# Border tiles first in the logit pass, and a weighted pass with four buffers, in a graph network on one Trainium2 core

## The reference

```python
q, k, v = (x @ Wq + bq), (x @ Wk + bk), (x @ Wv + bv)      # each (n, 8, 16)
e = (edge_attr @ We).reshape(-1, H, C)
alpha = einsum('ehc,ehc->eh', q[dst], k[src] + e) / sqrt(C)
amax = segment_max(alpha, dst, num_segments=n)
ex = exp(alpha - amax[dst])
denom = segment_sum(ex, dst, num_segments=n)
msg = (v[src] + e) * (ex / (denom[dst] + 1e-16))[:, :, None]
out = segment_sum(msg, dst, num_segments=n)
```

## Time and profile before

| | |
|---|---|
| median of 3 runs | 4402.17 us (4401.73 to 4405.57) |
| the profiled execution | 4408.67 us, span 4406.8 us, mean granted TensorE clock 0.815 |
| busy, share of the span | TensorE 65%, its weight loads 49%, VectorE 42%, ScalarE 10%, GpSimd 61% |
| logit pass | 3468 to 4001 us |
| segment max | 4001 to 4090 us |
| splitting | 4090 to 4112 us |
| weighted pass | 4112 to 4298 us |

### The profile page before, as it was taken

One profiled execution on the slowest core, in us unless ns is written; L12 is line 12 of the kernel. 1 busy time (PEld: TensorE's weight loads), 2 busy tenths in 40 slices (PEclk: granted clock), 3 DMA queues, 4 the chain that ended last, 5 costly groups with the idle time before them and its releaser, 6 DMA issues. The chain is left out here.

```text
span 4406.8 us, 65487 instructions
## 1 busy us (share of the span) xinstructions
PE 2876.3 (65%) x12218; PEld 2170.9 (49%) x12219; DVE 1830.9 (42%) x4838; ACT 421.2 (10%) x690; POOL 2678.7 (61%) x2816
## 2 busy tenths in 40 slices
PE   6555675555765568666677777766557665662687
PEld 3444444444444444444446666544444555652574
DVE  4222252222522226444453333422223666668764
ACT  2000020000200002000021111210001111110334
POOL 3777737777377773777727777367774477771000
PEclk9777797777977779778779999877777888886899
DMA  6222222222222222222212222122221355551340
GB/s 181 55 55 55 53 84 55 55 54 52 84 55 55 54 52 83 55 55 54 52 31 52 52 52 52 27 58 55 55 53 32 104 154 156 156 156 47 114 133 15
DMA packets 157822, 314.71 MB, mean 71 GB/s; under 512 B 58069, under 2 KB 79004, under 8 KB 157086
## 3 DMA queue, kind: packets, MB, share of 16 engines
q0 software_dynamic: 95744, 209.89, 18.4%
q1 hardware_dynamic: 55454, 101.15, 6.6%
q10 hardware_dynamic: 6400, 1.65, 0.2%
HBM read 250.84 MB, written 61.64 MB: 71 GB/s over the span
## 5 line engine op out<-in xcount | busy, mean ns | idle before, releaser
L595 POOL DMA_INDIRECT ring<-m_tab,idx x1568 | 1488.6, 949 | 720.1 <-issue 601.0
L1480 PE MATMUL ps<-oh,ring 128*128 128x256 f32 (+1 forms) x3328 | 963.6, 451 | 485.7 <-DMA ring<-m_tab,idx 380.6
L1480 PE MATMUL ps<-nodes,ring 128*128 128x256 f32 x2350 | 808.5, 509 | 475.1 <-DMA ring<-m_tab,idx 363.3
L1480 PEld LDWEIGHTS ps<-oh,ring 128*128 128x128 f32 x3328 | 703.2, 241 | 630.8 <-issue 528.0
L595 POOL DMA_INDIRECT ring<-x_tab,idx x795 | 754.9, 950 | 254.7 <-issue 244.3
L1480 PEld LDWEIGHTS ps<-nodes,ring 128*128 128x128 f32 x2350 | 575.6, 259 | 617.2 <-issue 516.4
L1018 DVE TENSOR_SCALAR oh<-iota,dl 128x256 f32<-128x256 f32 x1248 | 380.2, 375 | 951.4 <-PE ps L1480 943.3
L1018 DVE TENSOR_SCALAR nodes<-iota,dl 128x256 f32<-128x256 f32 x1183 | 361.8, 376 | 831.6 <-PE ps L1480 829.0
L595 POOL DMA_INDIRECT ring<-kv_tab,idx x416 | 399.2, 960 | 148.7 <-issue 126.5
L605 POOL TENSOR_TENSOR small<-small,bc 128x4 f32<-128x4 f32 (+1 forms) x28 | 31.1, 1109 | 597.4 <-DVE small L1118 597.4
L1480 PE MATMUL ps<-wpad,rts 128*128 128x128 f32 x832 | 162.8, 376 | 195.9 <-DVE pw L1270 195.9
(11 more groups left out here) (248 smaller groups left out, 2432.1 us busy)
## 6 DMA issues: line engine op xcount, KB each, us to landing
ring<-m_tab SPq DMA_DIRECT2D x2560, 0.5 KB
ring<-m_tab ACTq DMA_DIRECT2D x2560, 0.5 KB
ve_dr<-pw SPq DMA_DIRECT2D x52, 512.0 KB, 2.9
ring<-ve_dr SPq DMA_DIRECT2D x52, 512.0 KB, 3.4
ring<-m_tab,idx POOLq DMA_INDIRECT x1572, 2.6
m_tab<-ring SPq DMA_DIRECT2D x75, 256.0 KB, 2.2
ring<-x_tab,idx POOLq DMA_INDIRECT x796, 2.4
ring<-x_tab SPq DMA_DIRECT2D x640, 0.5 KB
```

The source lines that it names most:

```text
L595: pool.indirect_dma_start(rows[:, j, :], None, table, bass.IndirectOffsetOnAxis(ap=idx[:, g * WV + j:g * WV + j + 1], axis=0)).then_inc(ga ...
L1480: return T.matmul(o, lhsT, rhs, start=start, stop=stop, skip_group_check=True)
```

## The change

- **Order of the logit pass.** The waves 48 to 51, which hold the border copies, come first, written out (`logit_turns`); the loop then runs over waves 0 to 47. `alE` is filled with zeros first, and VectorE adds the scaled logits to what is there. At the end of each turn of the loop VectorE reads two tile numbers and adds two border slots to their tiles, in place of the 24 additions behind the loop. All engines and the gathers follow the new order.
- **Turned-over logits** are copied out of PSUM by ScalarE (`t_a`, `t_b`), and VectorE only scans. Eight fills become two of one column.
- **The weights of the border slots** are copied by GpSimd, behind its gathers; the last turn of the weighted pass waits for them (`ex_x`).
- **Splitting** is done turn by turn inside the weighted pass, for 32 slots, one turn ahead, in two buffers (`ex_parts`, `ex_rest1`, `ex_rest2`). ScalarE's copy of a wave's parts is gone. The reload of v + e waits for the last transposes of the weights only.
- **Weighted pass**: four buffers of one-hots and of their bf16 copies (`b_hot`, `ohb`); one-hots of a wave wait for the wave four before it. TensorE reads the sixteen column numbers of a wave from one row (`cols_b`, `load_both`). The loop's body holds two turns; the last three turns are written out. The two operations for `wbeta` stand behind the pass.

```diff
--- before.py
+++ after.py
@@ -88,10 +88,17 @@
...
+def load_both(pe, row, wave):
+
+    return pe.bass.values_load_multi_w_load_instructions(
+        row[0:1, ds(wave * (2 * WV), 2 * WV)], engines=[mybir.EngineType.PE], min_val=0, max_val=NP + (WIN - 1) * 24,
+        skip_runtime_bounds_check_because="window starts are multiples of 128 under 3200 by construction")[1]
...
@@ -182,9 +189,10 @@
...
-        cols24 = sb("cols24", [1, SLOTS], I32)
+        cols_b = sb("cols_b", [1, 2 * SLOTS], I32)
         tix = sb("tix", [1, 2 * EXTRA], I32)
-        basef = sb("basef", [1, SLOTS])
+        basef = cols_b[:, 0:SLOTS].bitcast(F32)
+        cols_v, cols_d = (cols_b[:, :].rearrange("p (g k j) -> p g k j", k=2, j=WV)[:, :, k, :] for k in range(2))
...
@@ -362,11 +375,11 @@
...
-        ohb = (pw[:, 2:4, :].rearrange("p a b -> p (a b)").bitcast(BF16)
-               .rearrange("p (b s c) -> p b s c", b=2, c=P))
+        ohb = (pw[:, :, :].rearrange("p a b -> p (a b)").bitcast(BF16)
+               .rearrange("p (b s c) -> p b s c", b=RING, c=P))
+        b_hot = ([oh[:, b, :, :] for b in range(2)]
+                 + [yT[:, 1024 * b:1024 * (b + 1)].rearrange("p (s c) -> p s c", c=P) for b in range(2)])
...
@@ -430,6 +443,25 @@
...
+
+        def logit_turns(eng, body):
+
+            for u in range(RING):
+                body(0, u, WAVES - RING + u)
+            with eng.Fori(0, TURNS - 1) as i:
+                for u in range(RING):
+                    body(i + 1, u, i * RING + u)
+
+        def weigh_turns(body):
+
+            def run(eng):
+                with eng.Fori(0, TURNS // 2 - 1) as i:
+                    for par in range(2):
+                        body(i * 2 + par, par, False)
+                for t in range(TURNS - 3, TURNS):
+                    body(t, t % 2, t == TURNS - 1)
+
+            return run
 
...
@@ -530,16 +562,16 @@
...
-            sp.wait_ge(s_dv, DV["ex_done"])
+            sp.wait_ge(s_pe, PE[f"exE{HEADS - 1}"])
...
@@ -583,18 +615,19 @@
...
+                    wave = (g - RING) % WAVES if single(k) else g
...
@@ -619,6 +652,15 @@
...
+            pool.wait_ge(s_dv, DV[f"ex{EX_DV - 1}"])
+            pool.wait_ge(s_ac, AC[f"ex{HEADS - 1}"])
+            for i in range(EXTRA // WV):
+                t = load_tiles(pool, tix, i, mybir.EngineType.Pool)
+                for j in range(WV):
+                    nc.gpsimd.tensor_copy(alE[:, i * WV + (TILES + j):i * WV + (TILES + j + 1), :],
+                                          alE[:, ds(t[j], 1), :]).then_inc(ex_x, 1)
+            nc.gpsimd.tensor_copy(alE[:, TILES + EXTRA:SLOTS, :], alE[:, 0:SLOTS - TILES - EXTRA, :]).then_inc(ex_x, 1)
...
@@ -771,16 +813,22 @@
...
+            act.wait_ge(s_dv, DV["t_z"])
+            for h in range(HEADS):
+                act.wait_ge(s_pe, PE[f"alT{h}"])
+                step(f"t_a{h}", nc.scalar.activation(alT[:, h * 512:h * 512 + 384], ps[:, h, 0:384], ACT.Copy))
+                step(f"t_b{h}", nc.scalar.activation(alT[0:TILES % P, h * 512 + 384:(h + 1) * 512],
+                                                     ps[0:TILES % P, h, 384:512], ACT.Copy))
...
@@ -790,20 +838,28 @@
...
+            def ex_parts(t, par):
+
+                if not isinstance(t, int) or t:
+                    act.wait_ge(b_used, t * RING)
+                if isinstance(t, int) and t == TURNS - 1:
+                    act.wait_ge(ex_x, EXTRA + 1)
+                nc.scalar.activation(ex3w[:, par, :, 0, :], alE[:, ds(t * TURN_S, TURN_S), :], ACT.Copy).then_inc(b_e0, 1)
+                act.wait_ge(b_r1, t + 1)
+                nc.scalar.activation(ex3w[:, par, :, 1, :], ex_rest[:, par, :, :], ACT.Copy).then_inc(b_e1, 1)
...
+            def weigh(t, par, last):
                 for u in range(RING):
-
-                    act.wait_ge(b_oh, i * RING + (u + 1))
-                    nc.scalar.activation(ex3w[:, u % 2, :, :], ex3f[:, ds((i * RING + u) * WV, WV), :], ACT.Copy)
-                    nc.scalar.activation(ohb[:, u % 2, :, :], oh[:, u % 2, :, :], ACT.Copy).then_inc(b_ohb, 1)
+                    act.wait_ge(b_oh, t * RING + (u + 1))
+                    nc.scalar.activation(ohb[:, u, :, :], b_hot[u], ACT.Copy).then_inc(b_ohb, 1)
+                if not last:
+                    ex_parts(t + 1, 1 - par)
+
+            ex_parts(0, 0)
+            weigh_turns(weigh)(act)
...
@@ -1245,69 +1303,75 @@
...
+            V.memset(alE[:, :, :], 0.0).then_inc(a_out, 1)
...
-                    V.tensor_scalar(alE[:, ds((i * RING + u) * WV, WV), :],
-                                    red[:, v, :].rearrange("p (s h) -> p s h", h=HEADS), 1.0 / HC ** 0.5, None,
-                                    ALU.mult).then_inc(credit, 1)
...
+                sums_ = alE[:, ds(wave * WV, WV), :]
+                dve.wait_ge(a_red, t * RING + (u + 1))
+                dve.wait_ge(a_v, g2 + 3)
+                if u == 0 and not isinstance(t, int):
+                    dve.wait_ge(a_out, t * 2)
+                elif isinstance(t, int):
+                    dve.wait_ge(a_out, 2)
+                V.scalar_tensor_tensor(sums_, red[:, v, :].rearrange("p (s h) -> p s h", h=HEADS), 1.0 / HC ** 0.5, sums_,
+                                       ALU.mult, ALU.add).then_inc(credit, 1)
+                if u == RING - 1 and not isinstance(t, int):
+                    tiles = load_tiles(dve, tix, t - 1, n=2)
+                    for j in range(2):
+                        if j == 0:
+                            dve.wait_ge(credit, (t + 1) * RING + before)
+                        dve.wait_ge(a_out, t * 2 + j)
+                        V.tensor_tensor(alE[:, ds(tiles[j], 1), :], alE[:, ds(tiles[j], 1), :],
+                                        alE[:, ds(t * 2 + (TILES + j - 2), 1), :], ALU.add).then_inc(a_out, 1)
...
-            for j, op in enumerate((ALU.add, ALU.subtract)):
-                step(f"wb{j}", V.tensor_tensor(wbeta[:, j, :], b_(f"L3_wbeta{j}").to_broadcast([P, P]),
-                                               b_("L3_wbeta2").to_broadcast([P, P]), op))
-
-            with dve.Fori(0, EXTRA // WV) as i:
-                t = load_tiles(dve, tix, i)
-                for j in range(WV):
-                    dve.wait_ge(a_out, i * WV + (j + 1))
-                    V.tensor_tensor(alE[:, ds(t[j], 1), :], alE[:, ds(t[j], 1), :],
-                                    alE[:, ds(i * WV + (TILES + j), 1), :], ALU.add).then_inc(a_out, 1)
-            dve.wait_ge(a_out, EXTRA + 1)
...
-                dve.wait_ge(s_pe, PE[f"alT{h}"])
-                step(f"t_a{h}", V.tensor_copy(alT[:, h, 0:384], ps[:, h, 0:384]))
-                step(f"t_b{h}", V.tensor_copy(alT[0:LAST, h, 384:512], ps[0:LAST, h, 384:512]))
-                after(f"t_b{h}")
+                dve.wait_ge(s_ac, AC[f"t_b{h}"])
...
@@ -1321,8 +1385,8 @@
...
-            for j in range(4, 12):
-                step(f"c_i{j}", V.memset(L8[j], -BIG))
+            step("c_if", V.memset(cf[:, 0:1], -BIG))
+            step("c_ib", V.memset(cb[:, 511:512], -BIG))
...
@@ -1372,31 +1436,45 @@
...
+            def ex_rest1(t, par):
+                if not isinstance(t, int) or t:
+                    dve.wait_ge(b_e2, t)
+                if isinstance(t, int) and t == TURNS - 1:
+                    dve.wait_ge(ex_x, EXTRA + 1)
+                dve.wait_ge(b_e0, t + 1)
+                V.tensor_tensor(ex_rest[:, par, :, :], alE[:, ds(t * TURN_S, TURN_S), :], ex3w[:, par, :, 0, :],
+                                ALU.subtract).then_inc(b_r1, 1)
+
+            def ex_rest2(t, par):
+                dve.wait_ge(b_e1, t + 1)
+                V.tensor_tensor(ex3w[:, par, :, 2, :], ex_rest[:, par, :, :], ex3w[:, par, :, 1, :],
+                                ALU.subtract).then_inc(b_e2, 1)
...
+            def weigh(t, par, last):
...
-                    g = i * RING + u
-                    sl = ds(g * WV, WV)
-                    dve.wait_ge(b_used, g + (RING - 1))
-                    one_hot(PASS_L3, i, u).then_inc(b_oh, 1)
-                    dve.wait_ge(b_ld[u], (i + 1) * 16)
+                    g = t * RING + u
+                    dve.wait_ge(b_used, g + 1)
+                    for j in range(0, WV, 2):
+                        ins = V.tensor_tensor(b_hot[u][:, j:j + 2, :], iota.unsqueeze(1).to_broadcast([P, 2, P]),
+                                              dl[:, ds(g * WV + j, 2)].unsqueeze(2).to_broadcast([P, 2, P]),
+                                              ALU.is_equal)
+                    ins.then_inc(b_oh, 1)
+                    if u == 0:
+                        ex_rest2(t, par)
+                    dve.wait_ge(b_ld[u], t * 16 + 16)
                     vv = ring[:, u, 0:WV // 2, :].rearrange("p a (s c) -> p (a s) c", c=HC)
-                    V.tensor_tensor(vv, vv, alE[:, sl, :].rearrange("p s h -> p (s h)").unsqueeze(2)
+                    V.tensor_tensor(vv, vv, alE[:, ds(g * WV, WV), :].rearrange("p s h -> p (s h)").unsqueeze(2)
```

(29 more changed lines are left out.)

198 lines of the change are left out of this document (92 added, 106 removed).

## The result

| | before | after |
|---|---|---|
| median of 4 runs of each | 4403.03 us (4401.73 to 4405.57) | 4359.51 us (4354.99 to 4362.24) |
| ratio | | 0.9899, 95% interval 0.9882 to 0.9917 |
| profiled execution: its own time, span | 4408.7, 4406.8 us | 4361.1, 4359.3 us |
| first gather of the logit pass starts | 3468.5 | 3468.9 |
| last scaling starts | 4001.1 | 4005.0 |

The prediction was 4330 us, with a range from 4318 to 4354. The two profiled executions are 47.5 us apart, and the timeline of after says where each part of that lies. Its columns are those of the earlier trace rows: start, duration, engine, line, operation, idle before.

The account below looks back on a forecast made before the run. GpSimd's issue bounds the logit pass, a VectorE chain the segment-max stretch, TensorE's queue the weighted pass. Terms -12.1 - 5.2 - 0.5 - 17.9 - 37.0 = -72.7 us give 4336 from the profiled 4408.7, 4330 by the median; range 4318 to 4354.

Parts of the forecast that it names:

- the load of sixteen numbers: TensorE's queue, weighted pass: one load per wave, 0.70 us at worst by 14 ns a number, 0.59 if count doesn't matter.
- the 2.79 us: Weighted pass: time TensorE's array alone needs for a wave, about 0.93 + 1.86.
- p = 3.47 less 0.74 for one load: Weighted pass: wave time p falls from 3.47 us by 0.74 for one load less; p taken as 2.83.
- The start of the pass: Weighted pass: first three waves run partly at a granted clock of 0.50, adding 2.2 us.
- The fill in the logit pass: Start of logit pass: zeroing the weights falls where VectorE waits for gathers; price 0, at most 3.0 us.
- the tail: After the logit pass's last wave: scaling-and-adding, one load and two additions replace the 24 additions; -12.1 us.
- the short chain: After the scans: fills shrink from eight to two of one column, but TensorE's transposes come late next; -0.5 us.
- the splitting: From ScalarE's last weights to the first small product: small product starts at about 4094.1 us; -17.9 us.
- the column numbers: Setup operations, two fewer and three more elsewhere, stand beside other work or waits: 0, bounds -0.7 and +0.5 us.
- Two loads stay: Rival, weighted pass: sixteen numbers need two loads of eight; term -3 instead of -37, time 4363 us; chance 11%.
- VectorE held by GpSimd's copies: Rival, weighted pass: GpSimd's 25 copies each hold up VectorE 1.01 us; term -15, time 4352 us; chance 12%.
- Numbers beyond eight one at a time: Rival, TensorE's queue: eight further numbers at 0.49 us each, load 4.5 us, time about 4530 us; chance 2%.

Follow-up runs that it names:

- the best version: Changed kernel with denominators 32 columns apart, eight numbers a wave, TensorE's turns written out, one-instruction one-hots and zeroing by ScalarE: median 4324.6 us, ratio 0.9828 to before.
- the ten loads: Changed kernel plus extra loads of 1 to 16 numbers in TensorE's queue: prices fit 0.06 us plus 0.26 us for each fetch.

## Why the prediction was wrong, by its steps

**The failed step is one term of the sum, the load of sixteen numbers.** It took "14 ns a number" from two rows, one number at 0.49 and eight at 0.59, and got 0.59 to 0.70; it is 1.10. Both rows are right, and the line through them is not: eight numbers are two fetches, and the one-number load is no unit of the same series (another single number took 0.32, so 0.49 held something else). With 0.51 more, the prediction's own lower figure of 2.78 becomes 3.29, and the 171.2 us measured are 52 x 3.29. That the two agree to the hundredth is partly chance: steady waves are 3.25, and the back edges make up the rest. The price was bounded by a straight line through two rows, and the range reached no further than that line. The weighted pass is 21.8 of the 25.2 us that are missing between the profiled executions: 24 from the wave (3.29 for 2.83), less 2.2 for a slow start that did not come.

**The bound was named right, and the 2.79 us beside it was half misread.** "TensorE's queue" gave the wave in every kernel but the two with one column for all small products. The 2.79 us put down to TensorE's array was 0.93 + 1.86. The 0.93 is the pace at which the queue dispatches the small products, which take 0.2 us up to the first large one when nothing holds them up; the 1.86 is real. As the time of a wave on TensorE with changing columns 2.79 was nearly right all the same: the best version has turns of 11.1 us, 2.78 a wave. But the two limits of 2.79 and 2.78 shared the dispatch of the small products, and a run was needed to see that TensorE alone could do 2.25.

**p = 3.47 less 0.74 for one load.** The 0.74 held the load and what stands around it. What the merge really spared was 0.28, the whole way from 3.53 to 3.25; with its two loads the new loop is no faster than the old one at 3.47, so the four buffers added nothing to the steady wave.

**The start of the pass**, +2.2 for the low clock: not seen. The first wave took 4.3 us at a granted clock of 0.50, 1.1 more than a steady one, and the second 2.4, 0.9 less, its numbers having been loaded while the first large products ran.

**The fill in the logit pass**, price 0, "at most 3.0 if it held up GpSimd's first issues": that is what it did, 2.5 us (4.14 to the second gather against 1.62 in before), and the start lay 0.4 later. The place was named and the wrong end taken. The reason given, that VectorE waits there, was about VectorE; the one to ask was GpSimd. The remaining 1.0 us of the +4.0 is spread over 414 gathers; it too is gone in the two traces in which ScalarE zeroes (532.6 us from the first gather to the last scaling in before, 536.1 in after, 532.7 in the last version). How the fill could reach that far the traces don't show, and two traces are few. The border additions in the turns stayed hidden, as said: VectorE still waits 154 us for gathers in the pass.

**What held**: the tail (1.68 us from the scaling to the last addition's end, 1.6 to 1.8 predicted), heads 2.23 us apart (2.25), the short chain, the splitting (first small product 3.64 us after the last weights, 3.9 predicted; first large one 1.03 later), the column numbers at 0.

**The rivals.** *Two loads stay*: there was one, with nearly the price of two; the time of that rival, 4363, was closer than the forecast. *VectorE held by GpSimd's copies*: out. GpSimd was busy 9.7 of the 10 us from 4077 to 4087, and VectorE's operations beside it took 1.42 and 1.22 us as everywhere. The copies took 0.4 us each and not 1.0 to 1.4, and were done by 4087, 140 us before ScalarE first read them. *Numbers beyond eight one at a time*: not so. Even at 0.26 us for each of the eight, the smallest step that the ten loads show, the load would have been 2.7 us, and it is 1.10.

**The two rules.** The Trainium skill, Runtime: NRT & Kernel Launch, section Instruction fetch mechanics, has about 200 ns per register. By the page's terms that is a load of registers from HBM, and the loads here read a row in SBUF, so the prediction applied the rule to a case that the page doesn't name. Sixteen took 1.10 us, 69 ns each, a third of the rule. It was nearer in kind than the prediction's line, since the price does rise with the numbers, but not evenly: fourteen cost more than sixteen. The Trainium skill, SBUF — State Buffer, section SBUF: two separate sides, in its box on DMAs issued by GpSimd, says that such a DMA can't write its descriptors while VectorE runs a fast-mode copy in SBUF. Here it was a fill, which the box doesn't name, and the first gather of 3.84 us beside a fill of 2.83 behaves as the box says. The prediction weighed that section's part on operations and left this box out.

## What to carry to other kernels

Where an engine waits with "issue" as the releaser, write down its queue, instruction by instruction: loads, register instructions, dispatches. Here 16 x 0.115 + load + 0.3 us (0.5 with two loads, 0.1 with the turns written out; 0.124 in place of 0.115 where each column takes one more step of arithmetic) gave the wave of the versions where VectorE didn't take over. Cutting it (eight numbers, denominators 32 columns apart, written-out turns) took another 25 us off the pass. Lay beside it what the engine itself does in order: from 2.97 us a wave down, TensorE's own sequence was as long as its queue's. Don't draw a line through two sizes of an operation. Of a moved fill ask what is being issued beside it. And where the profile names a releaser, look by its tiles whether that is the instruction the engine needed.
